# A two-layer transformer block on one core: first self-attention's output kept by feature, its dense stage rearranged, first cross-attention with fewer Pool jobs and joined transfers

## What is computed

```python
x = attn(ln1(x), ln1(x), Wq1, Wk1, Wv1) @ Wo1 + bo1 + x     # self-attention
x = attn(ln2(x), ctx,    Wq2, Wk2, Wv2) @ Wo2 + bo2 + x     # cross-attention, ctx: 8 x 64 x 192
a, g = split(ln3(x) @ Wff1 + bff1);  x = (a * gelu(g)) @ Wff2 + bff2 + x
attn: softmax(q k^T * 16**-0.5) v, head by head; out = concat of the 20 heads
```

## Time and profile before

| | |
|---|---|
| median of three runs | 3332.75 us |
| the profiled execution's own time | 3331.84 us |
| its span | 3330.1 us |
| PE busy | 2940.8 us (88%) |
| DVE busy | 2159.1 us (65%) |
| ACT busy | 1893.9 us (57%) |
| POOL busy | 808.3 us (24%) |
| mean granted TensorE clock | 0.841 |

### The profile page before, as it was taken

How to read it: one execution, slowest core, us unless ns; L and a number is a source line. 1 busy time by engine, 2 the same in 40 slices (tenths; PEclk the granted TensorE clock), 3 DMA queues, 4 the chain that set the end, 5 groups by cost and what they waited for, 6 DMA issues and landing times. The chain is left out here.

```text
span 3330.1 us, 47965 instructions
## 1 busy us (share of the span) xinstructions
PE 2940.8 (88%) x15582; PEld 1777.5 (53%) x15594; DVE 2159.1 (65%) x3834; ACT 1893.9 (57%) x3214; POOL 808.3 (24%) x1149
## 2 busy tenths in 40 slices
PE   6989999978796999998969999889979576899999
PEld 5754444457454888886841111111127332788888
DVE  5668888837353444444749999978868685444443
ACT  4338888845353232233549999999975355333322
POOL 2021222114640000000027878200003470200000
PEclk9979999989698999998975555555559888899999
DMA  8663333336662000001567566266722213010000
GB/s 229 211 167 101 108 106 103 90 81 162 162 177 47 10 10 19 9 0 32 152 174 167 125 143 138 58 91 91 96 49 97 80 45 92 26 36 18 25 17 16
DMA packets 358435, 296.57 MB, mean 89 GB/s; under 512 B 175794, under 2 KB 282106, under 8 KB 358250
## 3 DMA queue, kind: packets, MB, share of 16 engines
q1 hardware_dynamic: 348750, 274.52, 34.1%
q0 software_dynamic: 7280, 18.07, 2.1%
q10 hardware_dynamic: 2220, 1.70, 0.2%
HBM read 177.53 MB, written 114.52 MB: 88 GB/s over the span
## 5 line engine op out<-in xcount | busy, mean ns | idle before, releaser
L1599 PE MATMUL nat<-k_stack,q_stack 48*128 48x512 bf16 x640 | 383.6, 604 | 65.2 <-DMA k_stack<-k1w 23.6
L1395 DVE TENSOR_REDUCE neg_max<-nat 128x1 f32<-128x512 f32 x640 | 400.7, 682 | 59.7 <-PE nat L1254 59.6
L808 POOL TENSOR_TENSOR rstd<-var_eps,neghalf 128x4 f32<-128x4 f32 x48 | 51.9, 1082 | 1577.8 <-DVE var_eps L1032 1577.8
L1633 DVE TENSOR_REDUCE m_all<-nat 128x1 f32<-128x512 f32 x640 | 425.0, 691 | 13.8 <-PE nat L1599 13.5
L1653 ACT ACTIVATE nat<-nat,m_all 128x512 f32<-128x512 f32 x640 | 428.4, 2143 | 0.0
L1653 ACT ACTIVATION_READ_ACCUMULATOR nat<-nat,m_all 128x1 f32 x640 | 410.0, 1687 | 0.0
L1058 DVE SCALAR_TENSOR_TENSOR ff<-outp,bias,gel 128x512 f32<-128x512 f32 x160 | 120.1, 751 | 418.5 <-PE outp L326 418.5
L1329 ACT ACTIVATE probs<-sT 128x1024 f32<-128x1024 f32 x320 | 328.2, 1027 | 89.8 <-PE sT L1263 81.4
L972 ACT ACTIVATE gel<-outp,bias 128x512 f32<-128x512 f32 x160 | 110.2, 689 | 351.4 <-PE outp L326 351.4
L1852 ACT ACTIVATE exps<-sT 128x1024 f32<-128x1024 f32 x320 | 293.4, 1568 | 0.8 <-PE sT L1798 0.8
L976 ACT CAST ff_hi<-ff 128x512 fp32r<-128x512 f32 x160 | 99.2, 620 | 313.1 <-DVE ff L1058 313.1
(11 more groups left out here) (561 smaller groups left out, 7075.4 us busy)
## 6 DMA issues: line engine op xcount, KB each, us to landing
v<-vpad SPq DMA_DIRECT2D x64, 320.0 KB, 2.8
q_stack<-q_part SPq DMA_DIRECT2D x90, 160.0 KB, 5.9
k_stack<-k1w SPq DMA_DIRECT2D x90, 160.0 KB, 10.6
q_stack<-q_hi SPq DMA_DIRECT2D x160, 64.0 KB, 2.6
v_stack<-v SPq DMA_DIRECT2D x40, 256.0 KB, 3.2
q_stack<-q_hi SPq DMA_DIRECT2D x80, 128.0 KB, 2.8
raw<-v SPq DMA_DIRECT2D x16, 640.0 KB, 11.9
k_stack<-k_hi SPq DMA_DIRECT2D x158, 64.0 KB, 2.2
```

The costliest lines, as they stand in the source:

```text
L1395: dve.tensor_reduce(neg_max[:, n % 2, qt, 2 * pr + ab:2 * pr + ab + 1], nat[(16 * (n + 2) + t) % 3][:, :], AX.X, ALU.max, negate=True).the ...
L1599: pe.matmul(bank[i % NAT][:, :], q_stack[half, slot, g, pr, qt * P:(qt + 1) * P], k_stack[half, slot, g, pr, :], start=True, stop=True).th ...
L1633: dve.tensor_reduce(k.m_all[:, column(i // TILES, i % TILES)], bank[i % NAT][:, :], AX.X, ALU.max, negate=True).then_inc(s["e_max_ready"], 1)
```

## The change

**Self-attention.** The output is no longer turned or scaled. ScalarE copies `o_ps` to one of two halves of `o_sb`, SyncE stores all of its 128 rows (also the unused ones) by feature to `self_out`. The step `turn_output`, the copy to `o_turned`, the reciprocal and `norm` of each quad go, and with them their place in the `sT` ring. Once in five quads SyncE loads the 20 rows of sums of a sample (80 partitions of 128), VectorE inverts them in the middle of a quad's maxima, GpSimd splits the result into two parts, and SyncE stores these to `self_shares`. Sample 7's are done in the next stage (`LastShares`). SyncE doesn't wait at the end for its stores.

```diff
-                if exists(n - 2) and j == 2:
-                    uses["output", n - 2] = len(uses)
...
-                    if exists(n - 3):
-                        wait(sp, "a_o_normed", n - 2)
-                        sp.dma_start(rows(out, (n - 3) * TOK, TOK).rearrange("(t p) c -> p t c", p=P),
-                                     o_nat[:, (n - 3) % 2].rearrange("p t h c -> p t (h c)")
-                                     ).then_inc(s[f"a_o_stored{(n - 3) % 2}"], 16)
+                    if exists(n - 2):
+                        wait(sp, "a_o_copied", n - 1)
+                        sp.dma_start(rows(out, (n - 2) * P, P), o_sb[:, n % 2, :]).then_inc(s[f"a_o_stored{n % 2}"], 16)
+                    if exists(n - 3) and (n - 3) % QUADS == QUADS - 1:
+                        load_sums(sp, (n - 3) // QUADS)
+                    if exists(n - 6) and (n - 6) % QUADS == QUADS - 1:
+                        store_shares(sp, (n - 6) // QUADS, "a_recip_stored")
...
-                for r in range(2):
-                    wait(sp, f"a_o_stored{r}", 16 * (NQ // 2))
...
-                        if exists(n - 2) and j == 2:
-                            turn_output(n - 2)
...
-                        wait(act, "a_turn_full", output_use(n - 3) + 1 if n > 2 else 0)
-                        act.copy(o_sb[:, :], o_ps[:, :]).then_inc(s["a_o_copied"], 1)
+                        wait(act, f"a_o_stored{n % 2}", 16 * (n // 2 - 1))
+                        act.copy(o_sb[:, n % 2, :], o_ps[:, :]).then_inc(s["a_o_copied"], 1)
...
-                            act.copy(o_turned[:, n % 2, :], output_bank(n - 2)).then_inc(s["a_turn_free"], 1)
...
-                    if n >= 4:
-                        norm(n - 4)
+                    if n > 2 * QUADS and n % QUADS == 1:
+                        split_shares(pool, n // QUADS - 2)
...
-                        dve.reciprocal(recip[:, (n - 3) % 2], o[:, :, :, DH]).then_inc(s["a_recip"], 1)
...
+                        if t == 8 and exists(n - 4) and (n - 4) % QUADS == QUADS - 1:
+                            invert(dve, (n - 4) // QUADS)
```

```diff
+            if scale:
+                body = [("stats", 0), *scale[0:2], items[0], scale[2], oT[0], oT[1], items[1], oT[2], ("norm", 0), items[2],
+                        oproj[0], ("double", 0), zT[0], zT[1], oproj[1], zT[2], oproj[2], oproj[3]]
...
+                    if scale:
+                        heads = rows(attn_in, b * (QUADS * P), QUADS * P).rearrange("(h c) t -> c h t", c=VCOL)[0:DH]
+                        sp.dma_start(words(shares[:, :]), rows(recips, b * (2 * HEADS), 2 * HEADS)
+                                     ).then_inc(s["attn_in_loaded"], 16)
+                        for c in range(2):
+                            sp.dma_start(attn[:, c, :], heads[:, 8 * c:8 * c + 8]).then_inc(s["attn_in_loaded"], 16)
+                        for half in range(2):
+                            sp.dma_start(attn[64 * half:64 * half + 64, 2, :], heads[:, 16:HEADS]
+                                         ).then_inc(s["attn_in_loaded"], 16)
...
+                        bank_free(pe, st, b)
+                        pe.matmul(bank_of(st, r)[:, :], spread[:, m * P:(m + 1) * P], shares[:, :], start=True, stop=True
+                                  ).then_inc(s[turned[st][0] + "_full"], 1)
...
+                        bank_full(dve, st, b)
+                        dve.tensor_tensor(attn[:, m, :], attn[:, m, :], bank_of(st, r)[:, :], ALU.mult
+                                          ).then_inc(s[turned[st][0] + "_drained"], 1)
```

```diff
-                        for pr in range(2):
-                            act.dma_start(words(q_stack[QROWS:ROWS, (n + 2) % RING, pr, :]),
-                                          words(shift_sb[6 * pr:6 * pr + 6, n % 2, :])
-                                          ).then_inc(s[f"x_shift_loaded{n % 2}"], 16)
+                        act.dma_start(words(q_stack[QROWS:ROWS, (n + 2) % RING, :, :]), words(shift_sb[0:12, n % 2, :])
+                                      ).then_inc(s[f"x_shift_loaded{n % 2}"], 16)
...
-                    loader.turn(pool, n)
-                    if n < BATCH * TT:
-                        early.add(pool, n)
+                    if n % 4 == 3 and n // 4 <= len(loader.jobs):
+                        loader.turn(pool, n // 4)
+                    if n >= NQ - BATCH * TT:
+                        early.add(pool, n - (NQ - BATCH * TT))
```

More of the change, by code:

```diff
@@ L245, in start @@
             pool.wait_ge(self.s["pool_split"], self.split0 + j - 1)
[L246 to L248 removed]
+        if w.by_row:
+            for c in range(nch):
+                pool.dma_start(st[:, c, 0:nn], by_row(w.dram[(c0 + c) * P:(c0 + c + 1) * P, n0:n0 + nn])
+                               ).then_inc(loaded, 16)
+                self.counts[j % 2] += 16
+        else:
+            pool.dma_start(st[:, 0:nch, 0:nn], w.dram[c0 * P:(c0 + nch) * P, n0:n0 + nn].rearrange("(c p) n -> p c n", p=P)
+                           ).then_inc(loaded, 16)
+            self.counts[j % 2] += 16
         if w.rest:
             for half in range(2):
[L251 removed]
+                last = w.dram[w.full * P:w.K, n0:n0 + nn]
+                pool.dma_start(st[64 * half:64 * half + 64, nch, 0:nn], by_row(last) if w.by_row else last
                                ).then_inc(loaded, 16)
@@ L527, in dense_phase @@
         has_o = wo is not None
+        scale = [("scale", m) for m in range(3)] if recips is not None else []
         oT, oproj, zT = ([(x, m) for m in range(n)] for x, n in (("oT", 3), ("oproj", TT), ("zT", 3)))
@@ L555, in dense_phase @@
                 turned = {st: x for st, x in turned.items() if st[0] != "oT"}
+                turned.update({st: ("oT", st[1], 3) for st in scale})
             if not has_o:
@@ L1121, in dense_phase, with self_attention @@
             opening.passed()
[L1124 removed]
+def self_attention(nc, s, k, q, kk, v, out, recips, next_weights, bias):
     RING = 5
@@ L1224, in _ @@
                 load(1, k_stack, kk, (0, 1, 0))
-                for n in range(-2, NQ + 3):
+                for n in range(-2, NQ + 2):
                     if exists(n + AHEAD):
@@ L1375, in _ @@
                         early.add(pool, n)
-                for n in range(NQ - 4, NQ):
-                    norm(n)
+                split_shares(pool, BATCH - 2)
             @block.vector
@@ L1991, in _ @@
                 load_k(0, (1,))
-                for n in range(1, LOOK):
-                    load_q(n)
+                load_q(1)
                 wait(sp, "x_cleared", 2)
                 load_v(0)
-                for n in range(LOOK, RING):
-                    load_q(n)
+                for pair in range(2, PAIRS):
+                    load_q(pair)
                 load_k(1)
```

195 lines of the change are left out of this document (124 added, 71 removed).

## The result

Changed kernel: median **3320.8 us** of 20 runs, 3314 to 3332; the kernel before, on the same chip, 3332.0 (20 runs, 3327 to 3339). Two of the changed kernel's runs, at 4461 and 5465 us, count as slow: they are in the median, and in neither that range nor the ratio. Ratio 0.9967, 95% interval 0.9961 to 0.9974: 11 us faster, 9 to 13. Forecast were 24, so the sign and the range (3293 to 3325) hold and the size doesn't. The profiled execution took 3315.55 us, at the fast end of its own spread: its mean granted clock was 0.842, where the eighteen in that range average 0.840.

A forecast was written before the change was run, and what follows sets the result against it. The whole is 88% PE, but each of three changed stages has its own limit; -25.2 - 4.5 + 10.5 - 5.0 = -24.2 takes the profiled 3331.84 to 3307.6 us, median 3308 after adding 0.9; range 3293 to 3325.

The forecast's parts named there:

- Self-attention (-25.2): Self-attention: a quad takes 10.93 us instead of 11.58 without the turned output, 25.2 us less over all rounds.
- The walk through the waits: Self-attention quad: removing 0.59 us of PE shrinks VectorE's 0.74 wait to 0.15; about 0.36 of its 0.42 wait stays.
- Between the stages (-4.5): Self-attention to dense stage: first load 4.2 us earlier, then 5.4 us to PE, which starts 4.5 us earlier.
- Dense stage (+10.5): Dense stage: more VectorE work before norm makes a sample 17.0 us instead of 15.48, 10.5 us more over seven rounds.
- the ring: Dense-stage sample: statistics, normalization, turning, ScalarE's two forms three times, additions to x, next statistics; 15.48 us before.
- A rule against the change: Dense stage: VectorE operations with two SBUF inputs and GpSimd share a port pair; norm 2.67 us beside splitting, 2.05 without.
- Rival C: Dense stage: GpSimd blocks the low parts, 1.3 us a sample, +9 us in all, 3318; chance 0.10.
- Rival D: Dense stage: the clock falls to 1.2 GHz, +8 us a sample, 3364 if all seven; chance 0.04.
- Cross-attention (-5): Cross-attention: half of PE's waits for GpSimd go (4.6), larger first queries cost 1, last rounds save 1.4; -5 us.
- Rival B: Cross-attention: the clock rises earlier, sparing three rounds at 6.36 instead of 3.5 us, 8.6 us, 3300; chance 0.15.
- Feed-forward and the rest (0): Feed-forward: six loader jobs on an otherwise idle GpSimd, needed only by the third of ten chunks, cost 0.

The follow-up runs named there:

- pe_back: The changed kernel with two repeated matmuls in each quad of the self-attention, about where the turned outputs were; 3343.1 us.
- hold_loader: The changed kernel with GpSimd's loader work of a sample, DMAs included, taken only once VectorE's four norm instructions are done; 3317.7 us.
- combined_warm: combined with 32 transposes of the identity on TensorE, results unused, while it waits for the cross-attention's first queries and keys; 3300.3 us.
- combined: split_late with the cross-attention's first loads staged, later ones released by the copies of the first and second shift rows; 3295.1 us.
- split_late: norm_first with GpSimd's casts and subtractions held until VectorE's last low part of hT, the loader's DMAs issued ahead of norm; 3299.7 us.
- norm_first: The changed kernel with norm ahead of oT's high and low parts, and q's last output and two turnings ahead of the first oproj; 3328.3 us.

## Why the prediction was right and wrong

**Self-attention (-25.2): right, -23.9.** A quad of 10.93 us was 10.92. The walk through the waits had the mechanism (0.59 us of TensorE ahead of VectorE's next tile), and pe_back shows it by itself. In detail the 0.74 wait vanished altogether and the third wait kept 0.41 instead of 0.36.

**Between the stages (-4.5): nearly, -3.8.** The load went out 0.8 us behind the copy (0.7 said), but took 6.28 us to TensorE instead of 5.4.

**Dense stage (+10.5): the term that failed, +21.7.** The step was "With 2.6 for norm it ends at 9.9 ... ScalarE's first form follows 0.82 us behind, at 10.7". Measured in the sample above: norm starts at 748.65 - 741.04 = 7.61 (7.3 said); it takes 3.71 (2.6 said); the first form comes 1.38 behind its end (0.82 said), at 12.70. 0.31 + 1.11 + 0.56, less 0.11 in the rest of the ring, is 1.87 of the 1.9 us a sample that were missed. The ring itself was right, and the terms in it too small, norm's duration above all.

- The 0.31 is mostly the two low parts at 1.54 us instead of 1.28, which had been costed from a PSUM row although they read two SBUF tiles now.
- The 1.11 is GpSimd. The prediction moved norm by 2.3 us and kept the duration it had in the old place, when the earlier trace rows already showed two durations, 2.67 and 2.05. It read the 2.05 as norm without GpSimd's splitting beside it. The trace of before shows no cast beside it, but GpSimd isn't idle: in that last sample it issues two DMAs beside norm, whose four instructions take 0.45, 0.58, 0.84 and 0.43 us, and the first sample, with neither cast nor subtraction beside it, has 1.52. What lengthened the 2.05 isn't shown. Free, norm is 1.51 in the changed kernel too (hold_loader). The paragraph "A rule against the change" had the mechanism, though norm has one SBUF tensor input and not two, and the sum left it out.
- The 0.56 is the turning at half clock. ScalarE's first form waits for four transposes, and in the four samples whose turning keeps 1.00 it comes 0.90 to 0.92 behind norm, so 0.48 of the 0.56 is the clock. In three of these four the clock falls a little later, and they are as long. ScalarE's doubling of z (0.41 us) isn't in the way: it ends at 752.81, and ScalarE then waits 0.93 us for TensorE.

**Rival C** (0.10) had the mechanism and nearly the price, 3318, but named the low parts as the place, where 0.25 us fell, and not norm, where 2.2 did; that the price comes so near is in part luck, as other terms moved the time too. **Rival D** (0.04) happened in small: behind the gap of 2.23 us the clock falls for 3.4 us in five samples of six. A sample that kept 1.00 took 18.43 instead of 18.9 us, so 0.45 each and not 8. In hold_loader, where it stayed low for 10 us, two samples took some 4 us more.

**Cross-attention (-5): the size right, in part by luck.** By runs -7.3 (-10.7 to -4.0). GpSimd's waits went, nearly all 8 us of TensorE's and not half, but 4 to 5 us came back as a wait for the shift rows and 1.8 to 2.5 at the start (+1 said): the waits by themselves give little. **Rival B** (0.15) is what the changed kernel's first profile shows, but it is a draw: the rise came 17 to 46 us after the first product in fourteen profiles (combined_warm's by its second rise), and 21 with one and 27 with the other profile of the same kernel. What decides it is open, and so is whether the change makes an early rise more likely. What can be said is that combined, whose gaps in the first 17 us behind the first product add up to 1.3 us (5.6 in the changed kernel), rose after 17 and had the smallest spread, of only four runs.

**Feed-forward and the rest (0): right.** -0.6.

By the profiles, four of the five terms were good, and the fifth was missed by 11.2 us of the 24. The medians miss some 5 us more: the prediction put the median 0.9 us above the profiled execution, and it stands 5.3 above, with the lower mean clock of the runs (0.840 for 0.842). Where the 11.2 are was shown by getting them back: with norm first and GpSimd's work behind the last low part, seven samples take 111.3 us instead of 128.9, and the kernel 3299.7 us. combined, 3295.1 us (ratio 0.9884), beats both kernels.

## What to carry to other kernels

When a step is moved, cost it anew with the neighbours of its new place, on VectorE above all against GpSimd's instructions; a mean duration belongs to a place as much as to an instruction. Look at the neighbours of the rows that you price from, too: a duration from a row is free only if nothing of the other engine lies beside it. And when one engine's work is held back, leave the loads that it issues where they were: hold_loader's sample was 2.6 us shorter where nothing came in, and most of that was lost again to a load that came late and to the clock that fell when TensorE waited for it.

## What the runs showed of the hardware

- A group of VectorE instructions whose operands all lie in SBUF took up to 2.9 times as long beside GpSimd's subtractions (two low parts 3.76 us for 1.28, norm 3.71 for 1.51), and the scaling with its PSUM operand kept its 0.68 us. GpSimd pays too: its subtraction of 128x320 took 1.36 us where it started just behind a low part (748.11 and 748.05) and 0.86 in split_late.
- TensorE was busy for 18.00 of 18 us at a granted clock of 0.51 in the kernel before, and the time from the first product to the rise varied from 17 to 46 us over the profiles. In combined_warm the clock rose during work of no use and fell again 3.0 us into the useful work.
- Behind a gap of 1.28 us TensorE was at half clock for some 10 us (hold_loader), while gaps of 1.41 us in the samples of the changed kernel and 1.36 in those of norm_first_split left it at 1.00. The length of a gap alone doesn't decide.
